# Half of the squares in the second attention's way back moved from ScalarE to GpSimd

## The reference, cut to what matters

```python
def get_H(xx):
    z = xx @ W_fc.T
    e = jax.nn.sigmoid(jnp.concatenate([z[src], z[dst]], axis=-1) @ W_attn.T)
    ...
    w = jnp.exp(e - emax[dst])
    denom = jax.ops.segment_sum(w, dst, num_segments=n)
    h = jax.ops.segment_sum(w / denom[dst] * z[src], dst, num_segments=n)
    ...
dHdx = jax.grad(get_H)(x)
```

## Time and profile before

| | |
|---|---|
| median of 3 runs | 11343.61 us (11336.65 to 11345.05) |
| profiled execution, its own time | 11332.7 us |
| its span | 11330.9 us |
| busy, of the span | PE 44%, DVE 37%, ACT 26%, POOL 55% |
| first instruction of `back` on ScalarE | 9890.54 us after the span's start |

### The profile page before, as it was taken

The page is one execution under the profiler, slowest core; times in us unless marked ns, Lnnn a source line. Parts: engine busy times, 40 slices in busy tenths (PEclk is TensorE's granted clock), DMA queues, the critical chain, the costliest instruction groups (busy, mean ns, idle before and its releaser), DMA issues.

```text
span 11330.9 us, 88723 instructions
## 1 busy us (share of the span) xinstructions
PE 4971.7 (44%) x33461; PEld 2445.4 (22%) x33461; DVE 4153.9 (37%) x5350; ACT 2995.9 (26%) x2286; POOL 6231.1 (55%) x6250
## 2 busy tenths in 40 slices
PE   1000399800000577777556655344421530266655
PEld 0000288700000122222112121144420100112112
DVE  4555677610000000000067750088850003277730
ACT  0111100000000000000079950066630005399920
POOL 4777677767777777777770017788777660100000
PEclk5555555555555789998789986676765665599977
DMA  5666699970002999999954559755532963254568
GB/s 198 226 221 218 141 353 350 351 253 6 1 1 79 415 385 388 415 387 388 415 180 168 180 193 390 270 186 203 200 137 95 369 271 140 97 178 168 179 263 350
DMA packets 899556, 2664.78 MB, mean 235 GB/s; under 512 B 195270, under 2 KB 405303, under 8 KB 868644
## 3 DMA queue, kind: packets, MB, share of 16 engines
q1 hardware_dynamic: 670516, 2362.07, 54.6%
q0 software_dynamic: 213744, 171.80, 6.1%
q10 hardware_dynamic: 14976, 126.52, 2.7%
HBM read 1896.46 MB, written 763.47 MB: 235 GB/s over the span
## 4 chain that ended last, share of the span: by engine, by line
POOL 33%; DMA 19%; PE 14%; ACT 13%; issue 12%; ACTq 5%; DVE 3%; DVEq 1%; SPq 0%; POOLq 0%
POOL arena L416 16%; DMA arena<-cells_w 13%; POOL cells_w L419 7%; POOL xd L419 7%; ACT arena L720 6%; ACT arena L718 5%; ACTq L719 5%; PE ps L604 5%; PE ps L894 3%; DMA arena<-cells_c 3%; DMA xd<-arena 2%; POOL sorted L419 2%; PE ps L873 2%; PE ps L867 2%; ACT arena L528 1%
## 5 line engine op out<-in xcount | busy, mean ns | idle before, releaser
L604 PE MATMUL ps<-arena 128*32 128x400 f32 (+2 forms) x12200 | 2088.2, 698 | 2321.8 <-DMA arena<-cells_w 1660.4
L742 PE MATMUL ps<-arena 128*33 128x400 f32 x6400 | 1165.3, 507 | 751.6 <-DVE arena L733 751.5
L416 POOL DMA_INDIRECT arena<-t_a,arena x832 | 890.6, 1070 | 1066.3 <-DMA t_a<-arena 813.2
L604 PEld LDWEIGHTS ps<-arena 128*32 128x32 f32 (+1 forms) x12200 | 629.0, 150 | 3774.6 <-issue 2251.6
L419 POOL DMA_INDIRECT cells_t<-arena x832 | 887.1, 1066 | 291.0 <-issue 291.0
L419 POOL DMA_INDIRECT xd<-arena x832 | 872.2, 1048 | 256.3 <-issue 253.4
L419 POOL DMA_INDIRECT cells_w<-arena x832 | 809.1, 973 | 312.9 <-issue 272.1
L419 POOL DMA_INDIRECT sorted<-arena x832 | 813.7, 978 | 301.8 <-issue 287.9
L419 POOL DMA_INDIRECT cells_c<-arena x832 | 811.7, 976 | 297.1 <-issue 294.6
L416 POOL DMA_INDIRECT arena<-t_kv,idx x832 | 786.4, 945 | 257.8 <-issue 253.3
L1067 ACT ACTIVATE norm_cols<-norm_cols 128x1 f32<-128x1 f32 x5 | 1.0, 203 | 3400.1 <-DVE norm_cols L1049 3400.1
(11 more groups left out here) (467 smaller groups left out, 7437.9 us busy)
## 6 DMA issues: line engine op xcount, KB each, us to landing
arena<-cells_w SPq DMA_DIRECT2D x250, 3200.0 KB
arena<-cells_c SPq DMA_DIRECT2D x100, 3200.0 KB
cells_w<-arena SPq DMA_DIRECT2D x50, 3200.0 KB, 20.8
cells_c<-arena SPq DMA_DIRECT2D x50, 3200.0 KB
cells_t<-arena SPq DMA_DIRECT2D x50, 3200.0 KB
arena<-cells_c SPq DMA_DIRECT2D x100, 1600.0 KB, 6.5
arena<-cells_t SPq DMA_DIRECT2D x50, 3200.0 KB
arena<-cells_t SPq DMA_DIRECT2D x100, 1600.0 KB, 6.5
```

Source lines behind the costliest of these rows:

```text
L416: return pool.indirect_dma_start(dst, None, table, bass.IndirectOffsetOnAxis(ap=index, axis=0))
L604: last = pe.matmul(bank[base + k][g * f:(g + 1) * f, 0:m], own[:, t, :], TILE[b][:, g * width + at:g * width + at + m], start=t == 0, stop ...
L742: last = pe.matmul(bank[4 * kind + 2 * h + c][64 * g:64 * g + 33, 0:400], own[:, t, :], moving[:, at:at + 400], start=t == 0, stop=t == NT ...
```

## The change

In `back`, pieces with an odd buffer number (1 and 3, which is every second piece) are no longer squared by ScalarE. GpSimd squares them in place with a tensor_tensor multiply of `TANH[b]` by itself, once the exp has read it, and counts a new semaphore, `squared`, up. VectorE waits for that semaphore ahead of its second instruction on such a piece. `attend` is left as it was.

```diff
+        def squared_apart(name, b):
+
+            return name == "back" and b % 2 == 1
+
+        def squares_pool(pool):
+            for k, b, _, _, _, _ in pieces("back", (0, 1)):
+                if squared_apart("back", b):
+                    pool.wait_ge(S["weights_made"], k + 1)
+                    pool.tensor_tensor(TANH[b], TANH[b], TANH[b], ALU.mult).then_inc(S["squared"], 1)
...
-                act.activation(EXPO[b], TANH[b], ACT.Exp, scale=0.5, bias=half[:])
-                act.activation(TANH[b], TANH[b], ACT.Square).then_inc(S["weights_made"], 1)
+                last = act.activation(EXPO[b], TANH[b], ACT.Exp, scale=0.5, bias=half[:])
+                if not squared_apart(name, b):
+                    last = act.activation(TANH[b], TANH[b], ACT.Square)
+                last.then_inc(S["weights_made"], 1)
...
                 dve.drain()
+                if squared_apart(name, b):
+                    dve.wait_ge(S["squared"], k // 2 - NT * 2 + 1)
                 dve.scalar_tensor_tensor(TANH[b], TANH[b], -1.0, EXPO[b], ALU.add, ALU.mult).then_inc(S["weighed"], 1)
...
             ends_pool(pool, "dsum", OD, 64, DD)
+            squares_pool(pool)
```

## The result

The changed kernel takes 11410.42 us (11402.64 to 11416.34), the kernel before 11344.33 us (11336.65 to 11347.83), four runs each. The ratio is 1.0059, 95% interval 1.0041 to 1.0076: **slower by 66 us**. The direction and the place were as forecast; the forecast size was 166 us, and the time lies under the range of 11430 to 11615.

What follows compares the result with a forecast made beforehand. ScalarE was taken to bound `back`, VectorE after the change: 100 pairs of 10.92 us, 1092, plus 17.2 at the boundary, less 6.8, ending 166 us later; added to 11343.6, 11510 us, range 11430 to 11615.

Steps and rivals of the forecast that it cites:

- The bound of before and ScalarE's relief: In `back`, ScalarE sets the pace at 9.30 us a pair; one square fewer makes it 7.87, 1.43 us less.
- The exclusion: In `back`, GpSimd's square and VectorE's instructions with two SBUF operands shut each other out both ways: 10.92 us a pair.
- what a square takes from VectorE: In each pair of `back`, 3.42 us for GpSimd's square plus 0.1 for a hand-over each way, added to VectorE's 7.30.
- two hand-overs: In each pair of `back`, passing SBUF access from VectorE to GpSimd and back, allowed 0.1 us each.
- two and three streams: GpSimd's square in `back`, sized by SBUF reads and writes counted: 2.76 us for two, 4.08 for three; 3.42 taken.
- its sign of being wrong in size: Size is wrong if GpSimd's square in `back`, timed where VectorE rests at the phase boundary, is not near 3.4 us.
- the hole: VectorE's stop at the phase boundary of `back`, 17.2 us, with two squares inside it giving 6.8 us back.
- No exclusion: Rival for `back`: VectorE is never held by GpSimd, ScalarE stays the bound; 138 us less, 11206 us; chance 0.13.
- A cheap square: Rival for `back`: engines exclude each other, break-even square 1.83 us; one stream, 1.44 us, gives 11306 us; chance 0.04.
- The low end of the range: In `back`, two streams and half the hand-overs: 10.16 us a pair, 91 us later, 11435 us.
- The other signs: In `back`, ScalarE waits some 300 us for TensorE; GpSimd's squares take over 5 us when begun within a VectorE instruction.
- TensorE's clock: In `back`, TensorE was taken to stay at its upper clock level, 2.88 us a piece; the lower would add 20 us.

## Why the prediction was right in kind and wrong in size

**The bound of before and ScalarE's relief** were right: 1.43 us a pair was forecast, 138 us in all, and 137.5 is what came without squares.

**The exclusion** was right and decides the sign. It was read from one direction only, indirect DMAs of GpSimd held by VectorE. The other direction was an assumption: a VectorE instruction of up to 4.50 us where the longest had been 1.83. The changed kernel shows it, and the run with the sums of neighbours shows that it goes away when VectorE reads one operand. The Trainium skill's page "SBUF — State Buffer" (section "Who interferes with whom") has it that whichever of the two issues first keeps the other out for its whole instruction. The trace agrees up to 0.18 us where VectorE lost most: 2.67 of a square's 2.85, 3.39 of 3.56, 1.34 of 1.52. At the multiplication by 1.0 it is less: 3.09 of 4.24.

**The term that was mis-sized** is what a square takes from VectorE: 3.42 us and 0.2 for two hand-overs, 3.62 in all, taken for the middle of two and three streams. Measured, it is 2.65 to 2.67 in 64 of the 99 squares and 2.48 to 2.50 in 34. The two errors:

- The square is 2.85 us, not 3.42. The prediction named this as its sign of being wrong in size: GpSimd's time where VectorE rests was to be near 3.4, and the square at 10418.29, in the hole, took 2.85. Near enough to 3.42 is a product of two different tiles, 3.56 us. The count of streams took an instruction that reads one tile twice for one that reads two.
- The hand-overs cost nothing, and less than that: VectorE's lost time is 0.18 to 0.37 us shorter than the square.

The Trainium skill's page "GPSIMD Engine Reference" (section 3.1) has 4497 ns for an add of 2048 columns; the estimate of 3.5 us from it fits the 3.56 and not the square.

VectorE works from 9915.29 to 10917.26 + 1.83 = 10919.09, 1003.8 us, of which the hole is 10429.08 - 10411.90 = 17.2, as before. The 100 pairs are 986.6 us, 9.87 each: 9.95 where the first instruction is held, less where the second is. The forecast had 1092 - 6.8 = 1085.2. That is 98.6 less, and 166 - 98.6 = 67.4, the trace's 67.5. One smaller thing was wrong as well: one square falls into the hole, not two. The one ahead of it, at 10407.02, held the last L747 of the first phase. Why reading one tile twice is cheaper, no run here tells.

**The rivals.** "No exclusion" is refuted. Its gain, 138 us, came only with the sums of neighbours or when nobody squared. "A cheap square" puts the break-even at a square of 1.83 us, with its hand-overs 1.93. The runs fit that and don't pin it down: one that took up to 1.34 from VectorE gained, one that took up to 2.67 lost. The low end of the range had two streams, 2.76 us, and a hand-over of 0.1: 2.86. The square itself, 2.85, lies above its 2.76. What put the time under the range is the lost time that is shorter than the square. (200 x 4.65 is 930 us, not 929; nothing hangs on it.)

**The other signs.** ScalarE was to wait some 300 us for TensorE and waited 203.3, as goes with pairs of 9.87 us and not 10.92. GpSimd's squares were to reach over 5 us and reached 4.48.

**TensorE's clock** was granted at 0.87 over each phase in place of 0.98 and 0.99, so it was at the lower of its two levels (1.2 GHz) for longer than before. The prediction took that it stays. The time doesn't hang on it: in all of `back` VectorE is idle ahead of L741 for 15.5 us, once, waiting for the first counts, and ahead of L747 for 17.7 in small gaps, as before (8.7 in one phase); the hole is 17.2 in both kernels.

## What to carry to other kernels

Moving work to an idle engine helps only if it has its own way to the data. Where VectorE took both operands from SBUF, an instruction of GpSimd that read whole tiles there was paid for by VectorE: 2.67 of 2.85 us for the square, up to 3.09 of 4.24 for the product with a number. Ask first what the neighbour would pay to do the work itself (here 1.82 us against 2.67), and then move only as much as makes the two busiest engines even. In `back`, half of the squares on GpSimd lost 67.5 us, a quarter won 57.5, and a third on VectorE won 74.0.

## What the runs showed of the hardware that was not expected

- GpSimd's tensor_tensor on 128x1600 float32 took 2.85 us with one tile as both operands, and 3.56 us with two. A tensor_scalar multiply of the same size, with one operand, took 4.24.
- A VectorE instruction that is held by GpSimd is shown as a longer one (4.50 us), not as one that waits. Its group's mean (2612 ns) is the first sign.
- GpSimd's indirect DMAs are held by VectorE's instructions with two operands in SBUF: 1613 ns in the median against 969. With one operand in PSUM they are not (0.94 us within an L1272). In the other direction they cost nothing that shows: L729 never took over 1828 ns.
